# Decoder layer on one core: a new order of steps in the attention blocks, and four unread products at their seam

## The reference, cut to what matters

```python
q, k, v = (split_heads(x @ W + b) for W, b in ((Wq, bq), (Wk, bk), (Wv, bv)))
scores = einsum('bhqd,bhkd->bhqk', q, k) / scale
pos_k = rel_embeddings @ Wk + bk                      # 64 buckets of distance
c2p = take_along_axis(einsum('bhqd,hpd->bhqp', q, pos_k), c2p_pos, axis=-1)
p2c = take_along_axis(einsum('bhkd,hpd->bhkp', k, pos_k), p2c_pos, axis=-1)
probs = softmax(scores + (c2p + swapaxes(p2c)) / scale)
out = (probs @ v) @ Wo + bo + x
out = layernorm(out, eps=1e-7) * ln_scale + ln_bias
x = layernorm(x + out, eps=1e-5)
```

## Time and profile before

| | |
|---|---|
| median of 3 runs | 2842.94 us (2840.59 to 2843.41) |
| the profiled execution | 2838.59 us |
| its span, first to last instruction | 2836.9 us |
| busy: PE, DVE, ACT, POOL | 85%, 79%, 81%, 25% |
| mean granted clock of PE | 0.939 |
| attention stage | the first 950 us |
| of it, before the first scores | 85.5 us |

### The profile page before, as it was taken

The page is one execution under the profiler, slowest core; times in us unless marked ns, Lnnn a source line. Parts: engine busy times, 40 slices in busy tenths (PEclk is TensorE's granted clock), DMA queues, the critical chain, the costliest instruction groups (busy, mean ns, idle before and its releaser), DMA issues. The chain is left out here.

```text
span 2836.9 us, 64292 instructions
## 1 busy us (share of the span) xinstructions
PE 2414.7 (85%) x18180; PEld 1323.1 (47%) x18199; DVE 2232.0 (79%) x6591; ACT 2286.8 (81%) x4255; POOL 711.7 (25%) x565
## 2 busy tenths in 40 slices
PE   2888888888888337746699999999999999999997
PEld 1555555555555226614344444444444444444443
DVE  3788888788888576785488888888888888888887
ACT  1888888888888353317699999999999999999997
POOL 2334534544444101124311111111111111111114
PEclk7899999999999659977799999999999999999999
DMA  2000000000000100000011111211111121111113
GB/s 78 13 22 12 11 17 16 11 13 20 11 11 12 44 0 1 0 30 0 16 45 53 52 45 45 60 45 45 52 52 45 45 60 45 45 53 51 45 45 89
DMA packets 182540, 96.04 MB, mean 34 GB/s; under 512 B 22539, under 2 KB 179291, under 8 KB 182491
## 3 DMA queue, kind: packets, MB, share of 16 engines
q1 hardware_dynamic: 182491, 95.45, 12.0%
HBM read 78.10 MB, written 4.73 MB: 29 GB/s over the span
## 5 line engine op out<-in xcount | busy, mean ns | idle before, releaser
L1955 DVE TENSOR_TENSOR c_Hl<-c_HF,c_Hh 128x512 f16<-128x512 f32 x1028 | 679.6, 688 | 160.9 <-ACT c_Hh L1842 144.7
L1838 ACT ACTIVATE c_HF<-c_H,c_b 128x512 f32<-128x512 f32 x1028 | 711.0, 692 | 64.2 <-PE c_H L1777 44.3
L1842 ACT ACTIVATE c_Hh<-c_H,c_b 128x512 f16<-128x512 f32 x1028 | 706.4, 687 | 0.0
L1893 POOL TENSOR_TENSOR c_EX<-c_euler,c_D 128x16 f32<-128x16 f32 x65 | 188.6, 2902 | 1194.6 <-DVE c_D L1928 1194.6
L1775 PE MATMUL c_H<-c_Ch,SH 128*128 128x512 f16 x1028 | 390.1, 379 | 0.0
L1777 PE MATMUL c_H<-c_Ch,SH 128*128 128x512 f16 x1028 | 390.0, 379 | 0.0
L1776 PE MATMUL c_H<-c_Cl,SH 128*128 128x512 f16 x1028 | 390.0, 379 | 0.0
L1786 PE MATMUL c_Y<-c_Hh,SH 128*128 128x512 f16 x1024 | 388.1, 379 | 0.3 <-DVE c_Hl L1955 0.3
L1788 PE MATMUL c_Y<-c_Hl,SH 128*128 128x512 f16 x1024 | 388.1, 379 | 0.0
L1787 PE MATMUL c_Y<-c_Hh,SH 128*128 128x512 f16 x1024 | 388.1, 379 | 0.0
L692 DVE CUSTOM_DVE_ANT_0 a_T<-a_S,a_POS 128x128 f32<-128x128 f32 x1024 | 234.8, 285 | 48.0 <-PE a_S L436 41.0
(11 more groups left out here) (300 smaller groups left out, 4372.8 us busy)
## 6 DMA issues: line engine op xcount, KB each, us to landing
c_CWB<-c_rows SPq DMA_DIRECT2D x260, 256.0 KB, 4.1
a_QN<-a_QH SPq DMA_DIRECT2D x128, 32.0 KB, 1.9
a_KN<-a_KH SPq DMA_DIRECT2D x128, 32.0 KB, 1.8
out<-d_O SPq DMA_DIRECT2D x16, 256.0 KB, 2.3
a_QN<-a_QL SPq DMA_DIRECT2D x64, 32.0 KB, 1.9
a_KN<-a_KL SPq DMA_DIRECT2D x64, 32.0 KB, 1.8
CUR<-in_ctx SPq DMA_DIRECT2D x1, 1848.0 KB
c_rows<-c_CWR SPq DMA_DIRECT2D x65, 8.0 KB, 1.4
```

Source lines behind the costliest of these rows:

```text
L1838: act.activation(HF[:, k % 4, :], bH[k % 4][:, :], ACT.Gelu_apprx_tanh, bias=b1[:, g % EXPERTS, f:f + 1], scale=1.0 / WSCALE).then_inc(hf_ ...
L1842: act.activation(Hh[:, g % 2, f, :], bH[k % 4][:, :], ACT.Gelu_apprx_tanh, bias=b1[:, g % EXPERTS, f:f + 1], scale=1.0 / WSCALE).then_inc( ...
L1955: dve.tensor_tensor(Hl[:, g % 2, f, :], HF[:, k % 4, :], Hh[:, g % 2, f, :], ALU.subtract)\
```

## The change

In the steps of a block:

- PE makes K's product in step 2 and V's in four parts in steps 10 to 13; DVE's `values_in` moves from step 2 to 14, and the rounding of Q and K to steps 1 and 2 on ACT (behind the exponentials) and 2 and 3 on DVE.
- Bucket tiles: one each in steps 5 and 6, then two in each of 7 to 13.
- `second_norm` moves from step 9 to step 14. POOL's `residuals` no longer wait for it, but for the first normalisation.
- `EARLY_MAX` loses unit 6.
- QN and KN are counted by group, and a bucket tile waits for its own group's three DMAs.
- Behind the last position chunk PE issues four half-precision products of 128x512 into a bank that nobody reads before it is written anew.

At the start: x is loaded as its first four sequences, then four more, and the other 56 last; PE, ACT and DVE begin after the first ten loads; POOL copies block 0 as soon as its part of x is there and only then fills the rows of `table`, QN, KN and V.

```diff
-NORM_STEPS = (2, 3, 4, 5, 6, 7, 9)
+NORM_STEPS = (2, 3, 4, 5, 6, 7, 14)
+TILE_STEPS = (5, 6, 7, 7, 8, 8, 9, 9, 10, 10, 11, 11, 12, 12, 13, 13)
+V_STEPS = (10, 11, 12, 13)
-EARLY_MAX = range(6, 14)
+EARLY_MAX = range(7, 14)
...
+def tiles_of(u):
+
+    return [n for n, step in enumerate(TILE_STEPS) if step == u]
...
-                for src, dst in loads + late:
+                for src, dst in loads:
                     sp.dma_start(dst, src).then_inc(loaded, 16)
+                for n in range(2):
+                    sp.dma_start(X[:, n * NB:(n + 1) * NB, :], tokens[:, n * NB:(n + 1) * NB, :]).then_inc(x_in, 16)
+                    if n == 0:
+                        sp.wait_ge(x_in, 16)
+                for src, dst in late:
+                    sp.dma_start(dst, src).then_inc(late_in, 16)
...
-            def residuals(i):
-                hold(pool, spare_pool, link_s.sem, link_s.at(i, 0))
+            def residuals(i, first):
+                if not first:
+                    hold(pool, spare_pool, link_s.sem, link_s.at(i, -3))
...
-            pool.wait_ge(loaded, LOADS)
+            pool.wait_ge(x_in, 16)
             copy_block(0, 0)
+            pool.wait_ge(xb.sem, 1)
+            pool.memset(table[96:128, :, :, :, :], 0.0).then_inc(filled, 1)
...
-                if n == 0:
-                    pe.wait_ge(qn_in.sem, qn_in.at(i, qn_in.per * (1 + nxt)))
-                if n == 2 * NG:
-                    pe.wait_ge(kn_in.sem, kn_in.at(i, kn_in.per * (1 + nxt)))
+                if j == 0:
+                    done = (qn_in, kn_in)[kind][g]
+                    pe.wait_ge(done.sem, done.at(i, done.per * (1 + nxt)))
...
                     if u == 1 and not last:
-                        project_qk(i, 1)
+                        project_q(i, 1)
                     if u == 2 and not last:
-                        project_v(i, 1)
-                    for n in range(2 * (u - 6), 2 * (u - 6) + 2):
-                        if 0 <= n < TILES and not last:
+                        project_k()
+                    if u in V_STEPS and not last:
+                        project_v(V_STEPS.index(u))
+                    for n in tiles_of(u):
+                        if not last:
                             bucket_tile(i, 1, n)
...
+                    if u == UNITS + TAIL - 1 and not last:
+                        for _ in range(4):
+                            pe.matmul(bO[:, :], window[:, 0:P], table[:, 0, :, :, :].rearrange("p k j n -> p (k j n)"),
+                                      start=True, stop=True)
...
                     if u < UNITS:
                         exponentials(i, u)
+                    if u in (1, 2) and not last:
+                        high_half(i, 1, u - 1)
...
-                    if u == 1 and not last:
-                        low_half(i, 1, 0)
-                        low_half(i, 1, 1)
-                    if u == 2 and not last:
+                    if u in (2, 3) and not last:
+                        low_half(i, 1, u - 2)
+                    if u == 14 and not last:
                         values_in(i, 1)
```

More of the change, by code:

```diff
@@ L237, in attention_stage @@
                   (dr["bv"].rearrange("(a n) -> a n", a=1).to_broadcast([P, H]), bv_all[:, :])]
[L238 removed]
+        tokens = dr["x"].rearrange("b s h -> s b h")
+        late = [(dr["Wo"], Wo[:, :]),
                 (dr["bo"].rearrange("(a n) -> a n", a=1).to_broadcast([P, H]), bo_all[:, :]),
                 (dr["ln_scale"].rearrange("(a n) -> a n", a=1).to_broadcast([P, H]), scale_all[:, :]),
[L241 to L242 removed]
+                (dr["ln_bias"].rearrange("(a n) -> a n", a=1).to_broadcast([P, H]), bias_all[:, :]),
+                (tokens[:, 2 * NB:B, :], X[:, 2 * NB:B, :])]
+        EARLY, LATE = 16 * len(loads), 16 * len(late)
         @block.sync
@@ L293, in spread_keys @@
                     hold(pool, spare_pool, s_ps.sem, s_ps.at(i, UNITS))
-                hold(pool, spare_pool, qn_in.sem, qn_in.at(i, qn_in.per * (1 + nxt)))
-                hold(pool, spare_pool, kn_in.sem, kn_in.at(i, kn_in.per * (1 + nxt)))
+                for done in qn_in + kn_in:
+                    hold(pool, spare_pool, done.sem, done.at(i, done.per * (1 + nxt)))
                 pool.tensor_copy(QS[:, :, :, :], QN[:, :, :, :].rearrange("p g s b -> p g b s"))
@@ L356, in body @@
             def body(i, first=False, last=False):
+                if first:
+                    pool.wait_ge(x_in, 32)
+                    pool.wait_ge(late_in, LATE)
                 if not last:
                     copy_block(i, 1)
-                if not first:
-                    power(i - 1, 0)
                 for u in range(UNITS):
@@ L363, in body @@
                         take_max(i, u)
-                    if u == NORM_STEPS[5] and not first:
-                        power(i - 1, 1)
-                residuals(i)
+                    if u in (NORM_STEPS[1], NORM_STEPS[5]) and not first:
+                        power(i - 1, (NORM_STEPS[1], NORM_STEPS[5]).index(u))
+                residuals(i, first)
                 if not last:
@@ L386, in transposes, with project_q, project_k, project_v @@
                 last.then_inc(xT_ps.sem, 1)
-            def project_qk(i, nxt):
+            def project_q(i, nxt):
                 pe.wait_ge(xT_ok.sem, xT_ok.at(i, 1 + nxt))
                 pe.matmul(bG[0][:, :], Wq[:, :], xT[:, ::-1, :], start=True, stop=True).then_inc(qk_ps.sem, 1)
+            def project_k():
                 pe.matmul(bG[1][:, :], Wk[:, :], xT[:, :, :], start=True, stop=True).then_inc(qk_ps.sem, 1)
[L393 to L396, removed]
+            def project_v(b):
+                pe.matmul(bM[:, b * S:(b + 1) * S], xT[:, :, b], Wv[:, :], start=True, stop=True).then_inc(v_ps.sem, 1)
             def bucket_tile(i, nxt, n):
@@ L500, in _ @@
             pe.wait_ge(tab, 5)
-            project_qk(0, 0)
-            project_v(0, 0)
+            project_q(0, 0)
+            project_k()
+            for b in range(NB):
+                project_v(b)
             pe.wait_ge(tab, TAB)
@@ L562, in high_half @@
                 if nxt:
-                    done = (qn_in, kn_in)[n]
-                    act.wait_ge(done.sem, done.at(i, done.per))
+                    for done in (qn_in, kn_in)[n]:
+                        act.wait_ge(done.sem, done.at(i, done.per))
                 act.activation((QH, KH)[n][:, :], bG[n][:, :], ACT.Identity, bias=(bq, bk)[n][:, :])\
@@ L626, in body @@
                         x_columns(i, 1)
-                    if u == 1 and not last:
-                        high_half(i, 1, 0)
-                        high_half(i, 1, 1)
                     if 0 <= u - 3 < UNITS:
                         exp_columns(i, u - 3)
-                    for n in range(2 * (u - 6), 2 * (u - 6) + 2):
-                        if 0 <= n < TILES and not last:
+                    for n in tiles_of(u):
+                        if not last:
                             high_rows(i, 1, n)
@@ L656, in low_half @@
                 if nxt:
-                    done = (qn_in, kn_in)[n]
-                    dve.wait_ge(done.sem, done.at(i, done.per))
+                    for done in (qn_in, kn_in)[n]:
+                        dve.wait_ge(done.sem, done.at(i, done.per))
                 dve.scalar_tensor_tensor((QL, KL)[n][:, :], bG[n][:, :], (bq, bk)[n][:, :], (QH, KH)[n][:, :],
@@ L868, in body @@
                         norm_step(i - 1, NORM_STEPS.index(u))
-                    for k in range(2 * (u - 6), 2 * (u - 6) + 2):
-                        if 0 <= k < TILES and not last:
+                    for k in tiles_of(u):
+                        if not last:
                             split_rows(i, 1, k)
```

44 lines of the change are left out of this document (27 added, 17 removed).

## The result

The changed kernel takes 2901.29 us (median of 4 runs, 2898.97 to 2902.95), the kernel before 2842.01 beside it (4 runs, 2840.59 to 2843.41). The ratio is 1.0208 with a 95% interval of 1.019 to 1.0226: slower by 59 us. The forecast was 2892. One of the seven launches of the kernel before beside the first four experiments was slow (3595 us, mean granted clock 0.64), and every median here is of the fast ones.

What follows compares the result with a forecast made beforehand. No engine fills a block; PE, ACT and DVE wait for each other in turn. +5.1 us per block over 14 blocks (+71.4) and start-up -21.7 gave 2892 us, range 2797 to 2920, the forecast's own range 2872 to 2912.

Steps and rivals of the forecast that it cites:

- Start-up: Before block 0: waiting for ten loads instead of fifteen saves 15.9 us, three QN transfers instead of twelve 5.8; sum -21.7.
- Opening steps: First steps of a block: V's products leave step 2 and ACT reaches its exponentials earlier; -1.3 us per block.
- V's products: Steps 10 to 13: one product group returns in each at 0.5 us, part falling into a wait; +1.5 per block.
- The norm out of step 9: Step 9: without the second normalisation the step shrinks from 4.16 us towards its neighbour's 2.04; -2.1 per block.
- The 2.5 that the prediction named as a sign: In the changed profile, the step after unit 9's tiles should last near 2.5 us.
- The norm into step 14: Step 14: the four tensor_scalars alternate with POOL's seven back-to-back instructions, delaying unit 15 and the chunks; +7.0 us per block.
- The four products: Block's end: four unread products fill a 0.96 us gap, costing up to 0.2; cost and clock gain both taken as 0.
- the clock stays up: Possible gain from the four unread products: 0.8 us per block if the clock holds; not counted in the forecast.
- Rival 1: Step 14: the four go in one turn, so the kernel is faster, 2801 us or 2812 without the clock; chance 0.27.
- Rival 2: Step 14: V's products delay step 13's splits and the first pass meets QS; +2.2 per block, 2923 us; chance 0.13.
- Rival 3: Block's end: the stall is half absorbed by idle time of DVE and PE; +1.5 to +3 per block, 2842 to 2863; chance 0.10.
- Rival 4: Start-up: the reordering does not take hold because x is in the way; +4 us at most, counted inside the others.

Runs made afterwards that it cites:

- Experiment 6: Changed kernel with the second norm in step 16, POOL's residual sums before step 6, QS and KD after the norm, and most start-up fills before x's wait: 2779.1 us.
- experiment 1: Changed kernel with the second norm put back from step 14 to step 9, all else as changed: 2799.8 us.
- experiment 7: Kernel before with only the second norm moved from step 9 to 14 and the residual sums no longer waiting for it: 2940.0 us.
- experiment 2: Changed kernel with the second norm left in step 14, but POOL's residual sums, and so QS and KD, waiting until it is over: 2797.0 us.
- experiment 4: Changed kernel with each of the second norm's four 128x128 passes cut into two of 128x64, eight in all: 2967.3 us.
- experiment 3: Changed kernel without the four unread products behind the last position chunk: 2914.5 us.
- experiment 5: The kernel of experiment 2 (POOL waits for the second norm) without the four unread products: 2810.9 us.

## Why the prediction came out as it did

Its sign, its mechanism and its place were right. By its own steps:

**Start-up, predicted -21.7, measured -19.1.** DVE began at 9.84 (forecast 10.2), the large load of x was hidden, and the wait for three transfers in place of twelve was worth 5.7 of its 5.8 (from SP's first issue for QN to PE's first tile, 3.25 us for 8.97). What was missed lies between: from DVE's start to that first issue it now takes 22.8 us, 2.8 more. The prediction let POOL's fills end "before DVE comes to the table's last rows" and asked no more of them. But they run from 11.3 to 19.0, beside DVE, and two of the small fp32 tensor_scalars waited for the end of a fill of 1.8 us: 15.53 + 1.37 is 16.90, where the fill that began at 15.02 has ended (16.82), and 17.48 + 1.22 is 18.70, where the next has (18.68). That is 2.2 of the 2.8; the other 0.6 went before it, while PE's first products stood behind POOL's copy of block 0. Experiment 6 with the fills moved got 1.8 back. It is the same exclusion that the prediction charged in step 14 and did not look for here. Not every instruction pays: the tensor_tensor L833 took its usual 0.22 us beside the fill that began at 16.87. The Trainium skill, page "SBUF — State Buffer", section "SBUF: two separate sides", has this difference: a DVE instruction with two SBUF inputs competes only with a GpSimd instruction that reads SBUF, and a fill reads none; the trace agrees. A tensor_scalar of 128x1 at 15.21 (0.21 us as before) was not held up either; why is not shown.

**Opening steps, predicted -1.3, measured -1.3** (from block start to unit 8: 17.50 in the blocks of before that open at the full clock, 16.20 now). **V's products, predicted +1.5, measured +0.8** (unit 11's scores to unit 14's: 7.76 before, 8.53 in experiment 1), more of it falling into gaps than assumed. **The norm out of step 9, predicted -2.1, measured -1.1** (4.16 to 3.07; experiments 1 and 7 give the same): the prediction took as the step's natural length its neighbour's 2.04. But without V's products the steps from unit 8 on take 3.27, 2.04, 3.07, 2.16 and 3.26 us (experiment 7, block 5): they go by turns, and with the norm gone this one is a long one. The 2.5 that the prediction named as a sign did not come. The two errors nearly cancel: -0.3 for the part where -0.6 was said.

**The norm into step 14, predicted +7.0, measured +8.4** (unit 14's scores to the next block's, 18.93 to 27.3 on average). Its core, the stretch of the four, was said to be 5.6 us and is 6.79 - 1.11 = 5.7. Experiments 2 and 4 show the cause and the rule: no stream, no stretch; twice the instructions, further turns. The same placement without the stretch costs 0.85 (experiment 2 against 1: 17.57 and 16.72 from unit 15 on). The prediction had 7.0 - 5.6 = 1.4 for this part. What remains, 8.4 - 5.7 - 0.85 = 1.9, is the term that it left out: after the engines stood, the granted clock is low, and part of the chunks runs at 1.2 GHz. By stretch, in block 5:

```profile
402.00:412.00 10.00, 5.45 (x88) 3.70 (x88) 5.87 (x17) 4.93 (x13) 6.63 (x4) 0.50 0.00 0
```

From 401.78 it is low for 10.2 us. Over the blocks it is low for 6.8, 10.2 or 13.7 us, and unit 15's scores to the next block's take 24.5, 25.1 to 25.8, and 26.6: about 1 us more for each further 3.4 of low clock. That this is the clock's doing is argued from these lengths; no run held the clock up with the stall in place.

**The four products, predicted 0, measured -13 us in all.** The sentence that failed is "With PE idle for some 7 us before the chunks the clock will fall earlier, and I take 0 for both." The fall in the tail and the one at the seam are two. The clock does fall in the tail, and it is back at 1.00 well before the seam; without the four it falls again there (experiment 3). The price which the prediction had set aside for "the clock stays up" (0.8 per block) was the right one: 0.9 to 1.0 measured, with the stall (13.2 us) and without (13.9).

**Sum.** Per block -1.3 + 0.8 - 1.1 + 8.4 - 0.8 at the seam (10 of the 14 blocks of before opened at the low clock) is +6.0, predicted +5.1, measured +5.84; the difference of 0.15 is a second low clock that three blocks of before have between units 8 and 14 (17.96 us there instead of 17.24). The blocks 0 and 15 were put at 0 and gave 0.9 and 1.7 back. That the forecast was only 9 us low is in part luck. The start-up was too good by 2.6, the tail too cheap by 1.4 per block (20 us in all), step 9 and V's products together by 0.3 (4 us); against this stand the seam that it gave nothing (11 us of the block account) and blocks 0 and 15 (2.6).

**Rivals.** Rival 1, the four in one turn, did not happen; experiment 2 makes them go in one turn, and its 2797 stands near the 2801 worked out for that case. The long DVE run that kept a POOL copy out was no pattern for these instructions of 128 elements. Rival 2 (the first pass meets QS) did not come: the first ends at 398.47, when QS has just begun (398.34). The margin was as thin as was said, but the pass waited for the sum and then went ahead. Rival 3 falls: the blocks are 5.84 us longer and not 1.5 to 3, and in experiment 4 a longer stall makes them longer again. Rival 4 falls with the start-up.

## What to carry over

Before a DVE instruction is moved, look at what POOL has queued at the new place: in these runs a short group of tensor_scalars cost one POOL instruction for each of its own, so four passes of 0.26 became 6.8 us (DVE's copies of chunks were not held up, see below), and the remedy is a wait on the engine with slack (POOL), worth 104 us here for one line. Two gaps in which the clock falls are priced one by one; filling the one at the seam pays even when the other stays open. A step's own length without a piece of work is read from a step of the same kind in the same rhythm, not from the neighbour.

## What the runs showed of the hardware that was not expected

- The two engines alternated while DVE had fp32 tensor_scalars (R to X) queued and POOL its copy QS and its products KD, both in half precision: in experiment 4 six consecutive passes of 128x64 (0.30 us alone) took 0.69, 2.07 and four times 2.13, each until one POOL instruction had ended.
- Not every DVE instruction waits. The copies of the position chunks, which DVE reads from the banks that PE has written (a_POS<-a_S and a_POS<-a_G, 128x512), took 0.68 to 0.69 us each, all 104 of them that fell wholly inside KD's products in the trace of before.
- POOL does not lose by it: KD's four products take 8.28 us beside DVE's passes and 8.52 to 8.55 without them. All of the waiting is DVE's.
- A plain fill of POOL held up a tensor_scalar: one of 96x4 took 1.22 us for 0.16 beside the fill of 128x2048 (1.81 us), one of 128x128 took 1.37 for 0.23 beside the fill of 32x2048 (1.80).
- Four unread products of 128x512 in half precision, 1.04 us in a gap of 0.96, kept the granted clock at 1.00 at a seam where it fell to 0.50 for 3.4 us without them (all 15 seams in experiment 3, 12 of 15 in experiment 5). In experiment 7 the clock at the same seam stayed at 1.00 without them, after 10.2 us at the low level in the tail; why there and not in experiment 3 (6.8 us low in the tail) stays open.
